# A GNN kernel on one core: GpSimd's row gathers in spells of eight, each spell waited for before the next

## What is computed

```python
xn = _layernorm(x, axis=-1)
x = x + _L0_gnn_ref(xn, ..., src, dst, ...) + _L0_mix_ref(xn[None], ...)[0]
x = x + _L0_ffn_ref(_layernorm(x, axis=-1)[None], ...)[0]
xn = _layernorm(x, axis=-1)
x = x + _L1_gnn_ref(xn, edge_index, edge_weight, weight) + _L1_mix_ref(xn[None], ...)[0]
x = x + _L1_ffn_ref(_layernorm(x, axis=-1)[None], ...)[0]

# layer 0, graph attention over the edges (feat_src = sent_repr @ W_src, 4 heads of 64)
e = jax.nn.leaky_relu(el[src] + er[dst], NEG_SLOPE)
emax = jax.ops.segment_max(e, dst, num_segments=NW)
ex = jnp.exp(e - emax[dst])
den = jax.ops.segment_sum(ex, dst, num_segments=NW)
alpha = ex / den[dst]
msg = feat_src[src] * alpha[:, :, None]
rst = jax.ops.segment_sum(msg, dst, num_segments=NW)

# layer 1, weighted sum over the same edges
msgs = support[src] * edge_weight[:, None]
agg = jax.ops.segment_sum(msgs, dst, num_segments=N_NODES)
```

## Time and profile before

| | before |
|---|---|
| median of 3 timed runs | 1989.68 us |
| fastest and slowest of them | 1985.77 and 1990.58 us |
| span of the profiled execution | 2270.7 us |
| busy in it: TensorE | 1595.3 us, 70% |
| busy in it: VectorE | 1257.2 us, 55% |
| busy in it: ScalarE | 791.0 us, 35% |
| busy in it: GpSimd | 1083.0 us, 48% |

### The profile page before, as it was taken

How to read it: one execution, slowest core, us unless ns; L and a number is a source line. 1 busy time by engine, 2 the same in 40 slices (tenths; PEclk the granted TensorE clock), 3 DMA queues, 4 the chain that set the end, 5 groups by cost and what they waited for, 6 DMA issues and landing times. The chain is left out here.

```text
span 2270.7 us, 31260 instructions
## 1 busy us (share of the span) xinstructions
PE 1595.3 (70%) x7757; PEld 1248.9 (55%) x7757; DVE 1257.2 (55%) x3845; ACT 791.0 (35%) x2693; POOL 1083.0 (48%) x1198
## 2 busy tenths in 40 slices
PE   5525566666775876969999756877777877974792
PEld 4523344444444545858888644655555654753692
DVE  3524465655655785736667635555454454676335
ACT  2212454645455674635666430000000000121351
POOL 2562666666666301312112156666566666236441
PEclk9655677777777798979999777887888888986896
DMA  5642444444444206445444223333232233122786
GB/s 183 212 137 63 126 122 124 137 119 127 132 124 121 82 3 226 138 135 164 153 153 153 79 80 107 90 93 87 80 91 84 84 91 92 41 75 82 211 263 216
DMA packets 176878, 276.88 MB, mean 122 GB/s; under 512 B 28920, under 2 KB 132218, under 8 KB 176456
## 3 DMA queue, kind: packets, MB, share of 16 engines
q0 software_dynamic: 50352, 136.58, 20.9%
q1 hardware_dynamic: 82610, 94.62, 13.5%
q10 hardware_dynamic: 43750, 43.75, 5.8%
HBM read 202.35 MB, written 73.58 MB: 122 GB/s over the span
## 5 line engine op out<-in xcount | busy, mean ns | idle before, releaser
L487 POOL DMA_INDIRECT ring<-feat_d,src_lane x440 | 434.4, 987 | 277.5 <-issue 122.3
L1207 POOL DMA_INDIRECT rows<-xn_d,src_of x416 | 404.6, 973 | 244.9 <-issue 115.2
L1187 PE MATMUL bank<-ring,a_hot 128*128 128x260 f32 x880 | 309.6, 503 | 174.9 <-DVE ring L1086 89.3
L1378 PE MATMUL bank<-rows,big 128*128 x880 | 290.0, 445 | 140.4 <-DVE big L1286 79.0
L1187 PEld LDWEIGHTS bank<-ring,a_hot 128*128 128x128 f32 x880 | 205.2, 249 | 245.8 <-DVE ring L1086 107.6
L1116 ACT ACTIVATE ring<-ring 128x64 f32<-128x64 f32 x1320 | 322.7, 336 | 8.1 <-issue 7.3
L1295 DVE TENSOR_TENSOR big<-bank,big 128x256 f32 x440 | 186.7, 424 | 232.1 <-DMA m_bo<-in_L_mix_bo 111.3
L1378 PEld LDWEIGHTS bank<-rows,big 128*128 128x128 f32 x880 | 163.7, 209 | 241.1 <-issue 227.0
L1071 DVE TENSOR_TENSOR acc<-bank,acc 128x260 f32 x440 | 186.5, 424 | 145.7 <-DMA m_dst_bc<-dst_lo_d 72.5
L1348 ACT ACTIVATE big<-bank,a_col 128x256 f32<-128x256 f32 (+1 forms) x26 | 13.0, 552 | 415.1 <-PE bank L1393 263.5
L1286 DVE TENSOR_SCALAR big<-const,dst_lane,ew_lane 128x128 f32<-128x128 f32 x440 | 153.6, 350 | 1.0 <-PEq L93 1.0
(11 more groups left out here) (399 smaller groups left out, 2912.8 us busy)
## 6 DMA issues: line engine op xcount, KB each, us to landing
slots_d<-fold ACTq DMA_DIRECT2D x25, 1300.0 KB, 5.6
e_w_now<-in_L_ffn_w SPq DMA_DIRECT2D x56, 256.0 KB
a_dst_bc<-dst_lo_d SPq DMA_DIRECT2D x23, 512.0 KB
big<-in_L_ffn_W SPq DMA_DIRECT2D x16, 512.0 KB
e_x<-slots_d SPq DMA_DIRECT2D x56, 130.0 KB
ring<-feat_d,src_lane POOLq DMA_INDIRECT x440
rows<-xn_d,src_of POOLq DMA_INDIRECT x416
e_ys<-y_d SPq DMA_DIRECT2D x24, 256.0 KB
```

Source lines behind the costliest of these rows:

```text
L487: pool.indirect_dma_start(ring[:, q % RING, at, :], None, table, bass.IndirectOffsetOnAxis(ap=src_lane[:, n:n + 1], axis=0)).then_inc(gath ...
L1187: pe.matmul(bank[n % BANKS][:, 0:D + H], hot[:, q % HOTS, at, :], ring[:, q % RING, at, :], start=True, stop=True)\
L1207: pool.indirect_dma_start(rows[:, n % RING1, :], None, table, bass.IndirectOffsetOnAxis(ap=src_of[:, n:n + 1], axis=0)).then_inc(gathered[ ...
L1378: pe.matmul(bank[n % 4][:, 0:D], hot[:, n % HOTS, :], tile_of(rows, slots[n % 4]), start=True, stop=True)\
```

## The change

A constant `BURST = 8` and two helpers. `settled(pool, gathered, n)` makes GpSimd wait until all four gathers of step n's quad have landed (16 each, so 64 per turn of the ring); `arrived(pool, gathered, n)` until the gather of chunk n has. In each of the four loops over the gathers from step 32 on, GpSimd now calls one of them for the gather before, whenever n is a multiple of eight. The loop inside `node_projections` stays as it is. The number, order and targets of the gathers stay as they are, and so does what all other engines do.

```diff
@@ -60,6 +60,7 @@
 AHEAD = 2 * R
 UP_FIRST = 2 * MAXB // UP
 RING1 = 48
+BURST = 8
 PREFILL = 20
...
+def settled(pool, gathered, n):
+
+    q = n // 4
+    pool.wait_ge(gathered[q % RING], 16 * 4 * (q // RING + 1))
+
+
 def node_projections(nc, A, hold, bank, const, big_k, big_v, scores, dst_lane, src_lane, xn_d, xnT_d, feat_d, ring,
                      gathered, end_row, decay, link):
...
         @block.gpsimd
         def _(pool):
             for n in range(EARLY[NI + 1], BY_THEN):
+                if n % BURST == 0:
+                    settled(pool, gathered, n - 1)
                 gather_rows(pool, ring, gathered, src_lane, feat_d, n)
...
             for n in range(BY_THEN, NS):
                 if n % Q == 0:
                     once(pool, summed, n - RING * Q + Q)
+                if n % BURST == 0:
+                    settled(pool, gathered, n - 1)
                 gather_rows(pool, ring, gathered, src_lane, feat_d, n)
...
+def arrived(pool, gathered, n):
+
+    if n >= 0:
+        pool.wait_ge(gathered[n % RING1], n // RING1 * 16 + 16)
+
...
                 if n % 4 == 0:
                     once(pool, summed, n + 4 - RING1 + T - 1)
+                if n % BURST == 0:
+                    arrived(pool, gathered, n - 1)
                 fetch_rows(pool, rows, gathered, src_of, table, n)
...
             for n in range(PREFILL):
+                if n % BURST == 0:
+                    arrived(pool, gathered, n - 1)
                 fetch_rows(pool, rows, gathered, src_of, table, n)
```

## The result

The changed kernel takes 2220.9 us (median of 4 runs) against 1988.6 us for the kernel before: a ratio of 1.1169, interval 1.1148 to 1.1189. Measured again on one chip, side by side, it was 2218.2 against 1984.1, 1.1167 (1.1144 to 1.1191). It is slower by 232 us, where 137 were forecast, and it lies above the forecast range, which ended at 2159 us.

A forecast was written before the change was run, and what follows sets the result against it. The prediction took GpSimd's gather issue to bound both aggregations in timed runs. 94 waits at 1.7 us, 159.8 us, less 22.6 us of remaining old waiting, added 137.2 to 1989.7: 2127 us, range 1984 to 2159 us.

The forecast's parts named there:

- What bounds the kernel: Both aggregations: GpSimd's gather issue, 1.26 us each, sets the pace in timed runs, though the profile shows 14% waiting.
- Why the 281 us differ: Whole kernel: the profiled execution, 2270.7 us, is 281.0 us longer than the timed 1989.7; idle time shrinks in timed runs.
- The split by idle time: Both gather stretches hold half of TensorE's idle time, so they lose 141.4 of the 281.0 us.
- The waiting left over: Both aggregations: of GpSimd's 164.0 us of waiting, 22.6 us remain in timed runs to cover new waits.
- The price of a wait: Before every eighth gather: 1.7 us more than the 0.30 us issue gap, between 0.80 and 1.80; 159.8 us over 94 waits.
- The sum by the skill's figure: Aggregations: at the skill page's price of 1.06 us per wait, 77 us more, 2067 us in all.
- Nothing outside the aggregations: Mixer's stage and second prefetch: 10.2 and 3.4 us of waits are hidden and cost nothing.
- Both covers: GpSimd idle time, 41.85 us after the mixer's stage's last gather and 17.08 us at the second prefetch, hides their waits.
- (a): Aggregations: new waits take the place of old waits for ring room, 159.8 against 164.0; time 1990 to 1996 us; chance 0.15.
- (b): Aggregations: pauses without gathers in flight let consumers run faster, at most 25 us gained, 1965 us; chance 0.08.
- (d): TensorE waits longer and its clock stays low; above 2160 us only if landing takes over 2.10 us; chance 0.03.
- What I had said the profile would show: Gaps of 1.1 to 2.1 us at every eighth gather, others 0.30; profiled span within 20 us of before.

The follow-up runs named there:

- dose line: Waits at every 16th, 8th and 4th gather against the kernel before (1984.1 us): 2098.9, 2218.2 and 2455.9 us, 2.25 to 2.30 us per wait.
- delay_2: Kernel before plus a GpSimd power of 128x12 elements before every eighth gather of both aggregations, no landing waits: 2196.8 us, ratio 1.105.
- fewer: Kernel before without waits, every fourth gather left out from step 96 and chunk 48 on (178 gathers): 1840.6 us, ratio 0.928.
- early: Kernel before, no waits, with ten gathers more issued inside node_projections and ten fewer in the first aggregation: 1971.9 us against 1983.9, ratio 0.9939.
- the trace from chip 3: The kernel before, unchanged, traced on a chip where its median is 1987.7 us: span 1987.0 us, aggregation gathers 483.1 and 508.7 us.
- burst4: The changed kernel with a wait at every fourth gather in place of every eighth: 2455.9 us, 1.238 of the kernel before (1984.1 us).
- outside_3: Kernel before plus only the six waits of the mixer's stage and two of the second prefetch, on chip 3: ratio 1.0071, +12.7 us.
- outside: Kernel before plus only the six waits of the mixer's stage and two of the second prefetch, on chip 9: ratio 0.982, -38.5 us.

## Why the prediction was wrong, step by step

**What bounds the kernel: right.** In a timed execution GpSimd's issue is the pace of both aggregations, and its 14% of waiting in the profile shown is not there. The dose line, delay_2, fewer and early all agree with it, and the trace from chip 3 shows it.

**Why the 281 us differ: the reading was wrong, the number nearly right, and that by luck.** I took the profiled and the timed executions for the same execution, loaded and unloaded. They agree with executions on two kinds of chip; on either, the runs with a profile agree with the others. The split by idle time, for which nothing spoke, gave the two gather stretches 141.4 us; they lose 547.1 - 483.1 and 597.9 - 508.7, 153.2 us. The other half I had left unplaced. The mixer's stage loses 40.5 of it (94.4 by the earlier trace rows to 53.9), the prefetch 15.2, the tails 47.4 and 6.8, and the dense stage from 857 to 1310 us nothing: its 452.9 us stand against 451.1 on the quick chip.

**The waiting left over: 22.6 us forecast, 2 us measured** (1.4 and under 1). 20 us of the miss.

**The price of a wait: mis-sized, the largest term and the step that put the time outside the range.** Taken: 1.7 us, at most 1.80. Measured: 2.55 and 2.38 more than the 0.30 before. 45 x 2.55 + 49 x 2.38 = 231.4 us, net of what GpSimd waited before, where 159.8 - 22.6 = 137.2 stood. The landing was sized about right; what was missing is the second wait. Where a gather carries the landing wait alone, the idle time is the 2.10 us of the earlier trace rows: 2.07 to 2.12 us three times in the second half of the changed kernel's mixer's stage, and 2.01 and 2.12 in its second prefetch. In the aggregations `once` already waits before the same gather, and the compiled program then holds the landing wait as an instruction of its own on GpSimd's queue. By source line, `settled` and then `arrived` in the changed kernel (count, duration in ns, first and last start in us):

```profile
L495 POOLq EVENT_SEMAPHORE  x43: 17/17/17, 210.2 to 751.0; - x43
L1225 POOLq EVENT_SEMAPHORE  x49: 17/17/17, 1302.0 to 1903.9; - x49
```

It is 43 and not 45 because at n = 80 and 88 `once` does nothing. In the changed kernel's trace the landing and the next gather's start are 0.26 us apart where the wait stands alone and 0.74 where it has an instruction of its own (once 1.04), wherever the landing is on record. That is 0.48 us for each of 92 waits, 44 us. burst4 has both forms in one stage, at n = 80 and 84, where `once` does nothing, and at n = 96, the first with both waits:

```profile
194.87 0.95 POOL L488 DMA_INDIRECT ring<-feat_d,src_lane  x1 [2.12 <-DMA ring<-feat_d,src_lane]
201.96 0.95 POOL L488 DMA_INDIRECT ring<-feat_d,src_lane  x1 [2.11 <-DMA ring<-feat_d,src_lane]
...
224.22 0.95 POOL L488 DMA_INDIRECT ring<-feat_d,src_lane  x1 [2.62 <-DMA ring<-feat_d,src_lane]
```

Between them, at n = 88 and 92, stand 2.65 and 2.52 us with a single wait, where the gather itself landed late (3.21 us after its start at n = 92). Load does not explain the half microsecond: the second prefetch moves 92 GB/s and has gaps of 2.01 and 2.12 us, the second aggregation moves 87 and has none under 2.46. The other 18 us of the 62 by which 231.4 exceeds 94 x 1.80 = 169.2 are such late landings, with idle times up to 4.25 and 6.43 us; whether traffic delays them was not tested. No run takes away the wait for room and keeps the other, so the 44 us rest on these rows alone.

That the earlier trace rows gave 2.10 us, the value of a single wait, was partly luck. The same gather and the same cast are 1.45 to 3.81 us apart in the twenty traces of this case, and the gather was not alone either: gathers start 1.3 us before and after it. The Trainium skill, "DMA: Bandwidth & Descriptors", section "Anatomy of one DMA", would have 2.31 us from the issue to the landing, an estimate; the pages of the changed kernel and of chip 3 have medians of 2.8 and 2.9. The sum by the skill's figure, 77 us, was further off than the row's.

**Nothing outside the aggregations: wrong.** Both covers, the 41.85 and 17.08 us of idle, belong to the slow chip. On the quick one GpSimd's last gather of the mixer's stage is followed after 1.17 us by the first of the aggregation:

```profile
160.70 0.95 POOL L487 DMA_INDIRECT ring<-feat_d,src_lane  x1 [0.30 <-issue]
162.82 0.95 POOL L487 DMA_INDIRECT ring<-feat_d,src_lane  x1 [1.17 <-POOLq L93]
```

so GpSimd ends that stage and the eight waits are paid: 10.6 and 2.8 us by the windows, 12.7 by outside_3. The prediction named what it would cost with the cover gone, 10 us, and did not ask whether the cover was there in the timed execution, though it asked just that of the aggregations.

**Added up:** 231.4 for the waits in the aggregations, less 9.0 us of GpSimd's busy time (371.9 to 364.5 and 379.5 to 377.9), less 7.3 and plus 0.6 us in the tails, and plus 13.4 outside: 229 of the 232.3 us measured. The two traces are of different executions, so a few us of each term may be theirs.

**The rivals.** (a), cover by the old waits, is true of slow chips: 94 pauses cost 0.3% there. (b), faster by rest for the consumers, occurs there too, in the two stages I had excluded: 38.5 us less in outside, of which the mixer's stage has 29 (63.9 us against 93) and the second prefetch 8 to 10 (38.9 us against 47 to 49). (d) came nearest, time above 2160 with more than 2.10 us between a gather's end and the next start, and had too small a chance; most of the excess is not in the landing, to which it put it. What I had said the profile would show is half right: gaps of 1.1 to 2.1 us were forecast, most in the aggregations are 2.5 to 3.0; the span was to be that of before within 20 us, and it is 49.7 shorter, equal to its own timed 2220.9. That by itself would have told that a profiled execution takes no longer than the timed ones and that the profile of before came from elsewhere.

## What to carry to other kernels

If the profiled span and the median of the runs differ by more than the runs differ among themselves, the trace is of another execution than the times: stages whose cover, idle time or waits the argument rests on must then be priced with and without it, all of them, the small ones too. A producer that never waits (next to no real waiting behind `issue`) sets the pace whatever its busy share says (77% here), and each wait on it costs its full length. A wait on the producer's own last DMA has two parts: the time until it lands, of which one row is a poor sample (1.45 to 3.81 us here), and the time from there to the next start. For the second, count the waits that the instruction already has: beside a second one the new wait cost 0.48 us more each time.

## What the runs showed of the hardware

**Two kinds of chip, apart mainly where gathers run.** Same program, same bytes. The dense stages take 452.9 us against 451.1 and the last stages, with the experts, 280.7 against 277.0; the mixer's stage, the second prefetch and the two aggregations take 18 to 75% longer on the slow kind. There TensorE's results reach the others late while GpSimd issues gather after gather. The extreme is in the mixer's stage of the trace of before. TensorE's last product before it, ScalarE's next instruction, which waits for that, and TensorE's next:

```profile
152.93 0.42 PE L837 MATMUL bank<-const,acc 128*128 128x128 f32 x1
...
179.85 0.28 ACT L808 ACTIVATE m_ek<-bank 128x128 f32<-128x128 f32 x1 [26.91 <-DMA ring<-in_x]
...
181.75 0.45 PE L826 MATMUL bank<-const,m_dst_wide 128*128 128x128 f32 x1 [28.40 <-DVE m_dstT L754]
```

From 153.4 to 179.85 us nothing but GpSimd works; its last gather there ends at 175.4. In windows, the trace of before and then the quick chip's:

```profile
140.00:160.00 20.00, 3.44 (x16) 2.26 (x16) 3.43 (x11) 1.98 (x6) 15.12 (x17) 0.50 0.43 119
160.00:175.00 15.00, 0.00 (x0) 0.00 (x0) 0.00 (x0) 0.00 (x0) 11.34 (x13) 0.50 0.40 107
175.00:195.00 20.00, 9.91 (x45) 7.08 (x45) 12.40 (x46) 5.42 (x19) 0.39 (x1) 0.50 0.14 38
```

```profile
140.00:160.00 20.00, 17.88 (x80) 13.31 (x79) 6.84 (x25) 3.92 (x14) 15.13 (x17) 0.50 0.39 106
160.00:175.00 15.00, 4.30 (x13) 2.58 (x13) 9.45 (x29) 9.69 (x18) 10.79 (x12) 0.50 0.68 201
175.00:195.00 20.00, 18.31 (x87) 12.93 (x85) 15.43 (x44) 16.41 (x69) 15.43 (x16) 0.95 0.55 152
```

With a pause after every eighth gather (outside, chip 9) the standstill is gone and the stage takes 63.9 us in place of some 93 in the other three kernels of that chip. What holds TensorE's results back, and why on two chips of five, was not found; no run here isolates it. That is open.

One difference between the kinds is on record and has no explanation here. All nine traces from the slow kind hold 18,670 to 20,682 semaphore records, the eleven from the quick kind 30,801 to 33,746, though instructions and DMA packets are complete in both. They are missing where the gathers run: some 250 per 50 us against 950 in the first aggregation of the two traces of the kernel before, but about 500 in both in the dense stages. For this reason the page of before has no landing time for the gathers, and that of chip 3 has one:

```profile
ring<-feat_d,src_lane POOLq DMA_INDIRECT x440, 2.9
rows<-xn_d,src_of POOLq DMA_INDIRECT x416, 2.8
```

Whether the same cause delays the results and loses the records, or whether the recording, which every run here has, is itself what slows these executions, no run can say.

**A wait on the last gather is 2.0 to 2.1 us after that gather's end where it stands alone and about 2.5 where the next gather waits for something else too**, without late landings, and a wait that is met costs nothing that can be measured (102 of them: 0.04%, interval -0.1 to 0.2%).
